# Perceiver block on one core: how the first iterations of the attention loop are ordered

## The reference

```
q = norm(x) @ Wq.T + bq ;  k = ctx @ Wk.T + bk ;  v = ctx @ Wv.T + bv       # ctx: 16 x 512 x 512
scores = q k^T / sqrt(512) ; only the 32 largest of each row are kept ; softmax
x = x + (softmax @ v) @ Wo.T + bo
x = x + wave(norm(x))      # k-feature * v, causal convolution with a damped cosine per head, heads mixed, gated
x = x + W2t gelu(W1t norm(x) + b1) + b2      # W1t, W2t: weights rounded to -1, 0, 1 by mean |w|
```

## Time and profile before

| | |
|---|---|
| median of three runs | 474.55 us |
| profiled execution | 475.07 us, of which 473.2 us are the span |
| busy in the span | PE 451.0 us (95%), DVE 322.2 (68%), ACT 253.2 (54%), POOL 226.7 (48%) |
| PE clock granted | 0.996 of full speed |
| DMA | 48.93 MB, mean 103 GB/s |
| q products end, loop starts | 48.7 us |
| iteration 1, 2, 3 start on PE | 61.02, 79.98, 100.25 us |

### The profile page before, as it was taken

How to read it: one execution, slowest core, us unless ns; L and a number is a source line. 1 busy time by engine, 2 the same in 40 slices (tenths; PEclk the granted TensorE clock), 3 DMA queues, 4 the chain that set the end, 5 groups by cost and what they waited for, 6 DMA issues and landing times.

```text
span 473.2 us, 6285 instructions
## 1 busy us (share of the span) xinstructions
PE 451.0 (95%) x2146; PEld 353.9 (75%) x2146; DVE 322.2 (68%) x582; ACT 253.2 (54%) x391; POOL 226.7 (48%) x265
## 2 busy tenths in 40 slices
PE   6999899899999999897899999999989999999996
PEld 2588555678888887686688888888768888888884
DVE  4899679698999999765898883655763322433223
ACT  1787958678888786663787546441551111211111
POOL 5803099489779776950000771334216653333330
PEclk9999999999999999899999999999999999999999
DMA  7997724254435334364561300000000000010002
GB/s 225 410 357 276 281 77 120 68 169 115 135 109 161 108 90 166 105 217 177 175 227 46 111 1 22 1 0 0 2 0 0 1 0 1 32 57 1 0 1 89
DMA packets 23326, 48.93 MB, mean 103 GB/s; under 512 B 2688, under 2 KB 2688, under 8 KB 22272
## 3 DMA queue, kind: packets, MB, share of 16 engines
q1 hardware_dynamic: 23296, 48.55, 30.9%
HBM read 46.44 MB, written 2.10 MB: 103 GB/s over the span
## 4 chain that ended last, share of the span: by engine, by line
PE 62%; DVE 25%; ACT 5%; issue 4%; POOL 1%; DMA 1%; DVEq 0%; SPq 0%; ACTq 0%; POOLq 0%
PE bank L1177 9%; PE bank L1179 9%; PE bank L1178 9%; PE bank L1582 6%; PE bank L1596 6%; PE bank L1598 6%; PE bank L1583 6%; DVE mt_lo L943 5%; DVE work L956 4%; PE bank L1192 4%; DVE mx L952 3%; PE bank L1184 2%; DVE s_t L963 2%; PE bank L1270 2%; DVE prob L1020 1%
## 5 line engine op out<-in xcount | busy, mean ns | idle before, releaser
L416 POOL TENSOR_TENSOR nat_lo<-ctxr,nat_hi 128x512 fp32r<-128x512 f32 x64 | 84.0, 1339 | 19.5 <-ACT nat_hi L598 19.1
L755 ACT ACTIVATE g<-bank,b1c 128x512 f32<-128x512 f32 x32 | 22.1, 690 | 91.2 <-PE bank L1598 91.2
L1157 DVE CAST g_hi<-g 128x512 fp32r<-128x512 f32 x32 | 13.7, 427 | 76.9 <-ACT g L755 76.8
L469 POOL TENSOR_SCALAR w2s<-w2t 128x512 fp32r<-128x512 int8 x32 | 19.9, 621 | 68.2 <-PE bank L1583 68.2
L1582 PE MATMUL bank<-w2s,g_lo 128*128 128x512 f32 x128 | 50.2, 392 | 1.8 <-DVE g_lo L1159 1.8
L1596 PE MATMUL bank<-xt_lo,w1s 128*128 128x512 f32 x128 | 50.8, 397 | 0.0
L1598 PE MATMUL bank<-xt_hi,w1s 128*128 128x512 f32 x128 | 50.7, 396 | 0.0
L1583 PE MATMUL bank<-w2s,g_hi 128*128 128x512 f32 x128 | 50.2, 392 | 0.0
L574 ACT ACTIVATE mt_hi<-bank 128x512 fp32r<-128x512 f32 x64 | 37.8, 596 | 18.7 <-PE bank L1348 18.3
L943 DVE TENSOR_TENSOR mt_lo<-bank,mt_hi 128x512 fp32r<-128x512 f32 x64 | 43.5, 680 | 5.5 <-ACT mt_hi L574 5.2
L1348 PEld LDWEIGHTS bank<-ident,ctxr 128*128 128x128 f32 x256 | 30.6, 141 | 12.8 <-issue 4.5
(11 more groups left out here) (233 smaller groups left out, 1203.3 us busy)
## 6 DMA issues: line engine op xcount, KB each, us to landing
ctxr<-ctx SPq DMA_DIRECT2D x64, 256.0 KB, 2.9
wab<-w1T SPq DMA_DIRECT2D x4, 1024.0 KB, 10.7
wab<-w2T SPq DMA_DIRECT2D x4, 1024.0 KB, 5.4
wgraw<-wgT SPq DMA_DIRECT2D x4, 1024.0 KB, 5.4
wst<-w1T SPq DMA_DIRECT2D x4, 1024.0 KB, 4.8
wst<-w2T SPq DMA_DIRECT2D x4, 1024.0 KB, 5.4
resid<-x SPq DMA_DIRECT2D x4, 512.0 KB, 6.4
out<-resid SPq DMA_DIRECT2D x8, 256.0 KB, 2.2
```

The costliest lines, as they stand in the source:

```text
L416: pool.tensor_tensor(nat_lo[:, par, c, :], ctxr[:, b % 4, c, :], f(nat_hi[:, par, c, :]), ALU.subtract).then_inc(nat_lo_ok, 1)
```

## The change

Four things are done in another order or another way. The bias vector is now the row sum of Wo^T's rows times bv, made on DVE, and summed over the partitions by one product with ones in bank 3; the vector is put in `xn[:, 1, :]`, and POOL adds it to one tile of `resid` in each iteration from 1 on. The first row of wvo is made in iteration 0, the second in chunks 1 to 3 of iteration 1, the third in chunks 4 to 7, the fourth in iteration 2 around `turn_prob(0)`; rows 0, 2 and 3 use bank 5, row 1 bank 4. `kern` is made in iteration 1. The coupling product goes ahead of the last q product; `mix_part` and the norm move with it, and `token_part(6)`, the `ctok` addition and the scales take other places. ACT does each `abs_part` one place earlier, and SP loads `wvraw` ahead of the last two loads of the |w| sums.

```
@@ wvo_bank, SP @@
+        def wvo_bank(d):
+            return bank[4 if d == 1 else 5]
...
                     for k in range(3, 2 * DC):
+                        if k == 2 * DC - 2:
+                            sp.dma_start(wvraw[:, :, :], rows(wv)).then_inc(wv_in, 16)
                         abs_load(k)
-                    sp.dma_start(wvraw[:, :, :], rows(wv)).then_inc(wv_in, 16)
@@ POOL @@
-            def attn_bias(ts):
-                for t in ts:
+            def attn_bias(t):
+                if 0 <= t < NT:
...
-                    pool.tensor_tensor(resid[:, t, :], resid[:, t, :], bias_x[:, :], ALU.add).then_inc(xres_ok, 1)
+                    pool.tensor_tensor(resid[:, t, :], resid[:, t, :], xn[:, 1, :], ALU.add).then_inc(xres_ok, 1)
...
-                if i == 0:
-                    attn_bias(range(NT))
                 nat_lo_part(i - 1, 1)
+                attn_bias(i - 1)
@@ ACT @@
-            first_xt((4, 5, 6, 7))
+            first_xt((4, 5))
+            abs_part(0)
+            first_xt((6, 7))
             act.wait_ge(qbias_ok, 1)
             q_part(0)
-            abs_part(0)
+            abs_part(1)
...
             q_part(6)
-            abs_part(5)
+            abs_part(6)
             q_part(7)
...
                                 act.wait_ge(ctok_ok, 1)
+                                act.wait_ge(xbias_ok, 1)
                                 act.wait_ge(mix_ok, 1)
                                 act.wait_ge(norm_ok, 1)
+                                act.wait_ge(kern_ok, 3)
...
                 mt_hi_part(0)
-                if i == 2:
-                    wvo_hi_part(2)
+                if i in (1, 2):
+                    wvo_hi_part(2 * i - 2)
...
-                mt_hi_part(6)
                 if i == 1:
                     wvo_hi_part(1)
+                mt_hi_part(6)
@@ DVE, ahead of the loop @@
+            def xbias_sum():
+                dve.wait_ge(wo_in, 16)
+                dve.wait_ge(qbias_ok, 1)
+                for o in range(DC):
+                    row_sum(sum_k, woraw, 2, o).then_inc(sums_ok, 1)
+                    dve.wait_ge(sums_ok, DC + o + 1)
...
+            for t in range(4):
+                token_part(t)
+            mix_part()
+            dve.wait_ge(cos_ok, 2)
-            dve.tensor_tensor(kern[:, :, :], targ[:, :, 0:T], tdec[:, :, 0:T], ALU.mult).then_inc(kern_ok, 1)
+            dve.tensor_tensor(habs[:, :, :], targ[:, :, T:CT], tdec[:, :, T:CT], ALU.mult).then_inc(kern_ok, 1)
...
+            xbias_sum()
@@ DVE, loop @@
-                if i == 2:
-                    wvo_lo_part(2)
+                if i in (1, 2):
+                    wvo_lo_part(2 * i - 2)
...
+                if i == 1:
+                    dve.tensor_tensor(kern[:, :, :], targ[:, :, 0:T], tdec[:, :, 0:T], ALU.mult).then_inc(kern_ok, 1)
                 mt_lo_part(1)
...
                 mt_lo_part(2)
                 if i == 0:
-                    xbias_part()
+                    token_part(6)
...
                 mt_lo_part(4)
                 if i == 0:
-                    mix_part()
+                    xbias_part()
                 top8(i - 1, 2)
                 mt_lo_part(5)
-                top8(i - 1, 3)
-                mt_lo_part(6)
                 if i == 0:
                     norm_part()
...
+                top8(i - 1, 3)
+                if i == 1:
+                    wvo_lo_part(1)
+                mt_lo_part(6)
...
-                    if p == 0:
-                        dve.wait_ge(xres_ok, NT)
+                    dve.wait_ge(xres_ok, p + 1)
@@ PE @@
             for n in range(3, 2 * DC):
+                if n == 7:
+                    pe.wait_ge(cpr_ok, 2)
+                    pe.wait_ge(qbias_ok, 1)
+                    pe.matmul(bank[4][:, 0:H], cpr[0:H, :], ident[0:H, 0:H], start=True, stop=True).then_inc(coup_ps, 1)
                 q_product(n)
             def x_bias():
-                for o in range(DC):
-                    ins = pe.matmul(bank[4][:, :], cols[:, 2, o:o + 1].to_broadcast([P, P]), woraw[:, o, :],
-                                    start=(o == 0), stop=(o == DC - 1))
+                pe.wait_ge(sums_ok, 2 * DC)
+                pe.wait_ge(q_ok, 2 * DC)
+                pe.matmul(bank[3][:, :], ones[:, :].to_broadcast([P, P]), sum_k[:, :], start=True,
+                          stop=True).then_inc(xbias_ps, 1)
...
             def wvo_step(d, vs):
+                if d == 0 and vs[0] == 0:
+                    pe.wait_ge(wo_in, 16)
+                    pe.wait_ge(wv_in, 16)
+                    pe.wait_ge(ctok_sum, NT)
+                if d == 1 and vs[0] == 0:
+                    pe.wait_ge(mix_ok, 1)
+                    pe.wait_ge(norm_ok, 1)
+                    pe.wait_ge(scale_ok, 1)
+                if d >= 2 and vs[0] == 0:
+                    pe.wait_ge(wvo_lo_ok, 1 if d == 2 else 3)
...
+                if i == 0 and j >= 5:
+                    wvo_step(0, ((0,), (1,), (2, 3))[j - 5])
                 if i == 1:
                     if j == 0:
+                        totals()
+                    elif j < 4:
+                        wvo_step(1, ((0,), (1, 2), (3,))[j - 1])
                     else:
-                        wvo_step(2, (3,))
+                        wvo_step(2, (j - 4,))
                 if i == 2 and j < 2:
-                    if j == 0:
-                        pe.wait_ge(wvo_lo_ok, 2)
                     wvo_step(3, (2 * j, 2 * j + 1))
...
                         if pair == 0:
-                            pe.wait_ge(wvo_lo_ok, 3)
+                            pe.wait_ge(wvo_lo_ok, 2)
...
                 score(g0 + 1 - ahead)
-                wvo_in_turn(i, 1)
                 if i == 2:
                     turn_prob(0)
+                wvo_in_turn(i, 1)
...
                 if i == 0:
-                    x_bias()
+                    norms()
                 chunk(3)
...
                 weigh(i - 2, 0, 1)
+                if i == 0:
+                    x_bias()
                 chunk(4)
```

More of the change, by code:

```diff
@@ L510, in wvo_hi_part @@
                 act.wait_ge(wvo_ps, d + 1)
-                act.activation(wvo_hi[:, d, :], bank[4 + d % 2][:, :], ACT.Copy).then_inc(wvo_hi_ok, 1)
+                act.activation(wvo_hi[:, d, :], wvo_bank(d)[:, :], ACT.Copy).then_inc(wvo_hi_ok, 1)
             def first_tiles(ts):
@@ L549, in _ @@
             act.activation(tdec[:, :, :], tdec[:, :, :], ACT.Exp, scale=-1.0).then_inc(cos_ok, 1)
-            abs_part(3)
+            abs_part(4)
             q_part(4)
@@ L893, in xbias_part @@
                 dve.wait_ge(bo_in, 16)
-                dve.tensor_tensor(bias_x[:, :], bias_x[:, :], bank[4][:, :], ALU.add).then_inc(xbias_ok, 1)
+                dve.wait_ge(ctok_sum, NT)
+                dve.tensor_tensor(xn[:, 1, :], bias_x[:, :], bank[3][:, :], ALU.add).then_inc(xbias_ok, 1)
             def mix_part():
@@ L903, in mix_part @@
                 dve.tensor_tensor(mix_lo[:, :], cpr[:, :], f(mix_hi[:, :]), ALU.subtract).then_inc(mix_ok, 1)
+            for t in range(4):
[3 more added lines that the diff above has]
+            dve.tensor_tensor(habs[:, :, :], targ[:, :, T:CT], tdec[:, :, T:CT], ALU.mult).then_inc(kern_ok, 1)
+            dve.wait_ge(kern_ok, 1)
+            absolute(habs[:, :, :], habs[:, :, :]).then_inc(kern_ok, 1)
+            xbias_sum()
             def norm_part():
                 dve.wait_ge(norm_ps, 1)
-                link(dve.tensor_reduce(rnorm[:, :], bank[4][:, 0:P].rearrange("p (h c) -> p h c", h=H), AX.X, ALU.add))
+                link(dve.tensor_reduce(rnorm[:, :], bank[4][:, P:2 * P].rearrange("p (h c) -> p h c", h=H), AX.X,
+                                       ALU.add))
                 link(dve.tensor_scalar(rnorm[:, :], rnorm[:, :], 1e-8, None, ALU.max))
@@ L913, in wvo_lo_part @@
                 dve.wait_ge(wvo_hi_ok, d + 1)
-                dve.tensor_tensor(wvo_lo[:, d, :], bank[4 + d % 2][:, :], f(wvo_hi[:, d, :]),
+                dve.tensor_tensor(wvo_lo[:, d, :], wvo_bank(d)[:, :], f(wvo_hi[:, d, :]),
                                   ALU.subtract).then_inc(wvo_lo_ok, 1)
@@ L919, in scales @@
                 dve.wait_ge(abssum_ps, 1)
-                link(dve.tensor_reduce(winv[:, 0:2], bank[5][:, 0:2 * DC].rearrange("p (n k) -> p n k", n=2), AX.X,
+                link(dve.tensor_reduce(winv[:, 0:2], bank[4][:, 2 * P:2 * P + 2 * DC].rearrange("p (n k) -> p n k", n=2), AX.X,
                                        ALU.add))
@@ L995, in _ @@
                 if i == 0:
-                    token_part(6)
                     token_part(7)
-                if i == 1:
-                    wvo_lo_part(0)
+                    dve.wait_ge(ctok_sum, NT)
+                    dve.tensor_scalar(ctok[:, :], ctok[:, :], qbias[:, DC:DC + 1], None, ALU.add).then_inc(ctok_ok, 1)
+                    dve.wait_ge(ctok_ok, 1)
                 if i == 2:
@@ L1252, in x_bias @@
-                ins.then_inc(xbias_ps, 1)
```

(31 more changed lines are left out.)

49 lines of the change are left out of this document (5 added, 44 removed).

## The result

The kernel after took 477.44 us (median of 8 runs, 476.62 to 480.37), the kernel before beside it 474.56 (8 runs): a ratio of 1.0066, 95% interval 1.0041 to 1.0091. It is slower by 0.66%, 2.9 us; 475.0 was forecast, and 2.9 us is outside the range. The profiled execution is the longest of the eight, 480.37 us with a span of 478.5 and a mean granted clock of 0.987; the seven others took 476.62 to 479.10.

What follows compares the result with a forecast made beforehand. PE was taken to bound the loop, with room only in iterations 0 to 2. Earlier scores were outweighed by the last column's wait, +0.5 us; bias adds counted 0. Median 474.55 + 0.5 = 475.0 us, range 473.3 to 476.6.

Steps and rivals of the forecast that it cites:

- First score 52.85: Iteration 0: the first score starts at 52.85 in place of 53.84, -1.0 us.
- `wvo_lo(2)` ends at 82.5: Before the last column: this DVE subtraction ends at 82.5 us, before 83.0, as POOL's `nat_lo` is only some 0.5 earlier.
- PE stands 2.1 ahead of the last column: Iteration 2: PE arrives near 80.4 and waits about 2.1 us for `wvo_lo(2)`, since column 3 reuses bank 5.
- `weigh` at 88.3: Batch 0's weighing on PE starts at 88.3 us, before 87.75, 0.5 later.
- my lower end (-0.7): Best case for the last column's wait: `weigh` at 87.0 with DVE's list earlier and `prob` at 0.68, -0.7 us.
- my value (+0.5): Sum taken for the last column's wait: `weigh` and the load of batch 7 each 0.5 us later.
- 16.7 per iteration: Attention loop from 118 us on: each iteration still takes 16.7 us, with PE busy throughout.
- the context wait near 107: PE waits for batch 7's first context load, which hangs on `weigh`; PE at 106.58 comes at 107.1.
- (A): Rival, chance 0.18: the earlier scores are carried on through the loop, -1.1 us, 473.4 us.
- (C): Rival, chance 0.27: POOL becomes the loop's bound, its 1.23 us slack getting 1.25; +1.6 to +2.1, 476.4 us.
- I count 0: Bias adds, one per iteration behind `nat_lo`, fit POOL's wait for `ln_ve`: 0 us, +0.57 without DVE's cover.
- the 1.87 us around the span: Profiled time of 475.07 us less its span of 473.2, taken to stay unchanged.

Runs made afterwards that it cites:

- the two variants with one: The kernel after with the last wvo column in bank 7, 475.86 us; the same with all bias adds in iteration 0 as well, 476.31 us.
- the first kernel: The kernel after, also run a second time unchanged: 477.17 us, ratio 1.0066.

## Why the prediction was wrong

Right, or right but for the size:
- **First score 52.85, a PE wait of 1.0 at 57.1, 0.6 for the scales, `s_t` 67.65.** Measured 52.72, 0.93 at 57.05, 0.43 and 67.58. The 2.58 us of products did turn into waits.
- **`mt_lo(12)` 73.4.** Measured 73.30.
- **`wvo_lo(2)` ends at 82.5, PE stands 2.1 ahead of the last column, `weigh` at 88.3.** It ended at 81.97, 0.5 earlier than I had it. `prob` ends 0.55 us behind the end of the `nat_lo` operation that it meets (79.97 behind 79.42 in before, 79.36 behind 78.81 in after), and POOL is 0.6 earlier, about as I had it. But I wrote that DVE's list is the old one from there on, and it is not: `wvo_lo(1)` stood behind `prob` and now stands ahead of it, where `prob` has to wait for POOL anyway. That is the other 0.5. The stand was 1.08 to 1.24, for a wait I did not name lay ahead of it: 1.72 to 1.95 for the context load at chunk 16 (0.54 before), which waits for POOL's `nat_lo` and came only 0.6 earlier where PE was there 2.0 earlier. At full clock `weigh` came at 87.5, between my lower end (-0.7) and my value (+0.5).
- **16.7 per iteration, and the context wait near 107.** Measured 16.66; PE waited 0.81 at 109.61, in a profile that is 3 us late there, and 0.29 at 106.34 in the one at full clock. Between the second and third turned `prob` every profile of after or a variant lost 1.0 to 1.8 of its lead, 0.35 to 1.6 of it in waits for such loads. The claim that the loop hangs on the first weighing held: in all 17 profiles beside that of before the offset of the third turned `prob` (near 116) is that of the first weighing within 0.6 us, with weighings from 3.8 earlier to 3.1 later. That is what stood against (A): its gain of 1.1 had to be there at the weighing, and 0.2 was. The variants that had 3.1 to 3.8 there carried it on.
- **(C), a POOL ring that lengthens the iterations**, was right in its side and nearly in its time (476.4), and wrong in its mechanism: the iteration took one add for nothing. Half of its sign came: from 118 us on POOL is idle ahead of `rstd` for 0.4 us at most, at 140.81 and 157.47 not at all, yet no iteration there is over 16.8 us but the one with the late load (17.21).

Wrong, in three steps of the sum:
- **"I count 0" for the bias adds, 0.57 once at most.** I priced them where POOL waits for `ln_ve`. The last one stands where POOL does not wait: behind eight `nat_lo`, ahead of `rstd` and the cut of `kern`. It goes into the chain whole, with some 1.1 us: between the last turned `prob` and the first down product the offset jumps by 1.0 to 1.3 in every profile with that add in iteration 8 (two kernels without the fall in iteration 2: -0.02 to 1.07, -3.00 to -1.94), and moves by -0.2 to 0.1 in the kernels without it.
- **The span's end was left out of the sum.** I wrote that the 1.87 us around the span stay, and took the end of the span itself as unchanged. Six more entries on DVE bring a fetch of instructions among the output transfers, 0.5 to 0.9 us. No row that I had looked at shows it.
- **PE's stands were priced at their length alone.** Of 35 executions of kernels with both stands in iteration 2 (14 of the kernel after, 13 of the two variants with only the adds moved, 8 of after with 24 memsets) 8 had a mean clock of 0.991 or less and took 478.45 to 480.77, 1.4 to 3.8 us above the median of the others; of 90 executions of all other variants none had (five of them with the two shorter stands put into before), nor of 79 of before beside them. On the mean that is 0.5 us; on the median of the kernel after it is 0.46 in its first eight runs and 0.18 in the next six. That both stands are needed together is not shown: the two variants with one (1.80 and 2.38 us) had 19 runs, none at 0.991 or less, but five of the second were at 0.994 or 0.995 and 2 us slow.

Sum: 1.1 + 0.7 + 0.3 - 0.2 (the first weighing) = 1.9 of the 2.7 to 2.9 measured. The other 0.8 to 1.0 is not placed for certain. The profile that the offsets are taken against took 475.07 us, 0.5 above the median of before, so they are too small by about that. And a late context load in the middle of the loop (PE waits 0.20 to 0.95 for it at 154 to 161) stands in 7 of the 14 profiles of after and its variants, in none of the four of before and its variants. It comes and goes by execution: of two profiles of the same kernel (adds in iterations 1 to 6) one has it, 0.80 us with a loss of 1.24, and one has not. The bias adds are not its cause, since the kernel with all of them in iteration 0 has the longest wait (0.95). What is, stays open: a fetch of instructions stands within 2 us ahead of each of these late loads, but there is one at 151 to 160 us in all 18 profiles, those without a wait included.

The Trainium skill (GPSIMD Engine Reference, "Key points") was used for (C): GpSimd shares its SBUF interfaces with VectorE and contends with operations that have two SBUF inputs or run in a 2-port performance mode. The trace agrees for one with two inputs: `kern` took 1.22 us alone and 1.58 at 65.59 beside POOL's adds in the kernel with all adds in iteration 0. What cost time was another operation, the `tensor_scalar` on 2 values for the scales (0.17 us alone, 0.90 beside the adds; PE's wait 0.43 against 1.17). It has one input, and no row tells whether it runs in such a mode. On the iteration none of this bore.

## What to carry to other kernels

Price a small operation that is spread over a loop at each of its places, the last and the ones behind the loop above all: seven of eight were free here, the eighth cost its full length. Where a saved product turns into a wait of PE, put other work of the chain into the wait; that, one bank not reused and the adds ended two iterations sooner turned +0.66% into -0.49%. A lead counts only at the place on which the loop hangs, here the first weighing. Compare the gap behind the last matmul too: it depends on where the program's length lets a fetch of instructions fall.

## What the hardware did that I had not expected

- A fetch of one packet of instructions (0.01 MB) among the last 1.05 MB of outputs goes with 0.5 to 0.9 us more behind the last matmul, in 12 profiles against six. Six entries more in one engine's program brought it there, 24 took it out.
- A new tile of 128 bytes a partition, declared ahead of the large ones, made 115 us of MLP 0.42 us longer (0.37%), evenly. Nothing but addresses changed for PE. Why is open.
- After PE's two stands (1.95 and 1.08 us in one profile, 1.93 and 0.84 in another) the granted clock was 0.50 for some 6.8 us, most of it with PE busy again, at a cost of 2.8 to 3.0 us; in another profile of the first kernel, with stands of 1.72 and 1.24, it stayed at 1.00. The same fall at the loop's end (0.51 over 197.80 to 201.30 in before) cost at most 0.2: what a lower clock costs depends on whether PE is what the others wait for.
